# ScalarE's copies of a run's sums come three steps sooner in its order, in both scan layers

## The reference

```python
def step(hst, inp):                       # layer 1, 32 states; layer 3 has 64
    dt_t, B_t, C_t, x_t = inp
    dA = jnp.exp(dt_t[:, :, None] * A)
    hst = hst * dA + dt_t[:, :, None] * B_t[:, None, :] * x_t[:, :, None]
    y = jnp.einsum('bdn,bn->bd', hst, C_t)
    return (hst, y)
_, ys = jax.lax.scan(step, h0, seq)       # once forwards, once backwards in time
y = jnp.swapaxes(ys, 0, 1) + Dp * x
return y * _silu(z) @ out_proj_W          # then residual, layer norm, MLP
```

## Time and profile before

| | |
|---|---|
| median of 3 runs | 4702.95 us (4702.31 to 4705.61) |
| the profiled execution's own time | 4704.16 us |
| its span, first to last instruction | 4702.4 us |
| busy: PE, DVE, ACT, POOL | 4441.0, 4156.6, 4096.6, 3930.7 us |
| mean granted PE clock | 0.982 of full speed |
| scans on DVE (L1974) | 3072, 1.20 us each |
| products on POOL (L2341) | 768, 4.57 to 4.58 us each |

### The profile page before, as it was taken

How to read it: one execution, slowest core, us unless ns; L and a number is a source line. 1 busy time by engine, 2 the same in 40 slices (tenths; PEclk the granted TensorE clock), 3 DMA queues, 4 the chain that set the end, 5 groups by cost and what they waited for, 6 DMA issues and landing times.

```text
span 4702.4 us, 83409 instructions
## 1 busy us (share of the span) xinstructions
PE 4441.0 (94%) x32940; PEld 3730.5 (79%) x32940; DVE 4156.6 (88%) x4037; ACT 4096.6 (87%) x6807; POOL 3930.7 (84%) x1046
## 2 busy tenths in 40 slices
PE   8989899899899998999999999999999999999998
PEld 4458788778788884458888888888888888888887
DVE  6668999999899986759999999999998999999997
ACT  3459899899899974459999999999999999999996
POOL 4429899889889984539999998999998999989996
PEclk8999999999999999999999999999999999999999
DMA  3001111111111121011121211211211212111111
GB/s 125 1 15 51 50 47 51 46 46 51 46 46 50 51 68 39 1 39 54 57 75 54 77 50 52 78 57 54 79 55 46 80 59 76 54 50 65 56 59 41
DMA packets 90085, 252.74 MB, mean 54 GB/s; under 512 B 12240, under 2 KB 26448, under 8 KB 89696
## 3 DMA queue, kind: packets, MB, share of 16 engines
q1 hardware_dynamic: 89696, 247.40, 15.2%
HBM read 243.70 MB, written 3.67 MB: 53 GB/s over the span
## 4 chain that ended last, share of the span: by engine, by line
PE 47%; ACT 35%; DVE 8%; POOL 6%; issue 4%; DMA 0%; DVEq 0%; SPq 0%; POOLq 0%; ACTq 0%
PE psum L1015 12%; ACT weights_c L1528 9%; PE psum L748 9%; PE psum L1001 9%; ACT work L1528 7%; ACT work L1543 7%; PE psum L998 7%; ACT weights_c L1543 5%; PE psum L1115 5%; POOL work L2341 4%; DVE work L1974 3%; ACT L1316 2%; PE psum L1191 1%; DVE weights_c L1974 1%; ACT weights_c L1545 1%
## 5 line engine op out<-in xcount | busy, mean ns | idle before, releaser
L2341 POOL TENSOR_TENSOR work<-work,weights_a 128x2048 f32<-128x2048 f32 x512 | 2331.7, 4574 | 281.2 <-DVE work L1974 279.5
L1974 DVE TENSOR_TENSOR_SCAN work<-weights_c,psum 128x512 f32<-128x512 f32 x1366 | 1571.0, 1201 | 115.2 <-PE psum L1001 99.0
L1015 PE MATMUL psum<-ident,work 128*128 128x128 f32 x8192 | 1239.3, 275 | 12.9 <-ACT weights_a L1342 8.3
L2341 POOL TENSOR_TENSOR weights_c<-weights_c,weights_a 128x2048 f32<-128x2048 f32 x256 | 1168.3, 4580 | 73.9 <-DVE weights_c L1974 73.4
L1528 ACT ACTIVATE work<-work,decay 128x504 f32<-128x504 f32 x1366 | 965.5, 707 | 52.0 <-DVE work L1974 22.8
L1015 PEld LDWEIGHTS psum<-ident,work 128*128 128x128 f32 x8192 | 971.0, 143 | 14.8 <-ACT weights_a L1342 9.2
L1001 PE MATMUL psum<-ident,work 128*128 128x128 f32 x5464 | 937.8, 274 | 0.0
L1974 DVE TENSOR_TENSOR_SCAN work<-work,psum 128x512 f32<-128x512 f32 x682 | 789.8, 1200 | 40.9 <-PE psum L1001 28.1
L1974 DVE TENSOR_TENSOR_SCAN weights_c<-work,psum 128x512 f32<-128x512 f32 x684 | 792.0, 1200 | 37.7 <-PE psum L1001 36.9
L1001 PE MATMUL psum<-ident,weights_c 128*128 128x128 f32 x3752 | 696.9, 275 | 0.0
L1001 PEld LDWEIGHTS psum<-ident,work 128*128 128x128 f32 x5464 | 672.5, 143 | 0.0
(11 more groups left out here) (192 smaller groups left out, 6393.8 us busy)
## 6 DMA issues: line engine op xcount, KB each, us to landing
weights_a<-c_rows SPq DMA_DIRECT2D x384, 512.0 KB, 3.6
weights_c<-in_L_cond_fwd_in_w SPq DMA_DIRECT2D x8, 512.0 KB, 6.4
weights_c<-in_L_cond_fwd_xproj_w SPq DMA_DIRECT2D x4, 1024.0 KB, 7.3
weights_c<-in_L_cond_bwd_in_w SPq DMA_DIRECT2D x8, 512.0 KB, 5.8
weights_c<-in_L_cond_bwd_xproj_w SPq DMA_DIRECT2D x4, 1024.0 KB, 7.8
x_stream<-in_x_t SPq DMA_DIRECT2D x4, 512.0 KB, 8.6
weights_a<-in_L_cond_w SPq DMA_DIRECT2D x2, 1024.0 KB, 15.0
weights_a<-in_L_cond_W SPq DMA_DIRECT2D x2, 1024.0 KB, 8.0
```

The source lines that it names most:

```text
L1015: last = nc.tensor.matmul(PS[:, t, j * P:(j + 1) * P], buf["ring"][s % RING][:, j, t * P:(t + 1) * P], IDENT[:, :], start=begins, stop=((s ...
L1974: v.tensor_tensor_scan(buf["ring"][s % RING][:, j, along], buf["decay"][q % DECAYS][:, along], PS[:, 4 + q % LOOKAHEAD, along], 0.0, ALU.mult,
L2341: g.tensor_tensor(state, state, buf["c"][:, s // 2 % 2, s % 2, :].unsqueeze(1).broadcast_to([P, DC, T]), ALU.mult).then_inc(ss["prod_ready ...
```

## The change

One number: the step at which ACT's copies are due goes from 9 to 6. DVE's copies stay at 9, and so does PE's order.

```diff
                 def copy_sums(r, yt, done):
-                    yield 9
+                    yield 6
                     made("pe", f"dtx3@{r - 2}")
                     act.wait_ge(ss["sum_done"], r * pl.states)
                     for t in (0, 1):
```

## The result

The changed kernel takes 4692.69 us (median of 12 runs, 4692.13 to 4694.78) where the kernel before, on the same chip and beside it, took 4703.53 (12 runs, 4702.11 to 4709.89). The ratio is 0.9975, with a 95% interval of 0.9967 to 0.9984: 10.84 us, 0.23%. The forecast was 4691, in a range of 4686 to 4698.

The account below looks back on a forecast made before the run. PE's waits for ACT's copies at four layer 3 boundaries stall DVE, which sets the pace: 13.4 us back, less 1.4 for PE's clock, other places nothing, makes 12.0 off the median of 4702.95, near 4691 us; range 4686 to 4698.

Parts of the forecast that it names:

- The four places: Layer 3, runs 1, 2, 4 and 6, where PE waits for ACT's copies: 13.4 us back, 1.4 staying, 12.0 gained.
- The new waits of ACT: Before its moved copies ACT waits 1.8 us in three layer 1 runs, 2.9 in three of layer 3; costed at nothing.
- A fall at three of the four places: PE's clock falls after its remaining 1.84 us gap at three layer 3 boundaries, 0.45 us each, 1.4 us kept lost.
- The rule of the Trainium skill: Short idle gaps between bursts of matmuls keep PE's clock up; if it held, nothing would stay and the gain be 13.4.
- POOL: Rival: POOL, busy without a break through the boundary, sets the pace; gain some 2.5 us, 4700 us; 10%.
- The lead in the ring of states: Reason against POOL: four states and late adds let DVE run some microseconds ahead of it without waiting.
- PE does stay slow: Rival: the clock falls at scan 10 anyway, later stalls of 2.2 us stay in runs 2, 4, 6; 4696 us; 15%.
- ACT starving the scans: Rival: in layer 1 and layer 3's odd runs the new wait outlasts its cover; 15 us slower, 4718; 4%.
- The factor of 1: Whatever idle time DVE does not lose at a boundary is won whole by the next boundary, microsecond for microsecond.
- cover 1.5 us: Layer 1: the input of step 16 is complete at 1060.0, PE wants it at 1061.5, so ACT's new wait costs nothing.
- ACT makes the 1.8 us good: Layer 1: ACT later idles before decays that wait for a scan, and recovers its new 1.8 us wait there.

Follow-up runs that it names:

- the four places alone: The changed kernel with ACT's copies at step 6 only in runs 1, 2, 4 and 6 of layer 3, step 9 elsewhere: 4692.99 us, ratio 0.9975.
- run 4: No follow-up kernel: a stretch of one layer, from its scan 0 to the next run's; in layer 3, 333.78 us before, 331.53 changed.
- step 7: The changed kernel with ACT's copies due at step 7 instead of 6: 4692.82 us, ratio 0.9976 to the kernel before.
- run 2: No follow-up kernel: a stretch of one layer, scan 0 to next scan 0; layer 1 169.67 us before, 170.91 changed; layer 3 335.51 before, 333.05 changed.
- step 3: The changed kernel with ACT's copies due at step 3 instead of 6: 4713.03 us, ratio 1.0021 to the kernel before.
- step 5: The changed kernel with ACT's copies due at step 5 instead of 6: 4697.9 us, ratio 0.9987 to the kernel before.
- three copies on ACT: The changed kernel with ACT copying three of the four banks and DVE one: 4684.14 us, ratio 0.9957 to the kernel before.
- run 0: No follow-up kernel: a stretch of one layer, from its scan 0 to the next run's; in layer 3, 307.96 us before, 308.25 changed.

## Why the prediction was right

**Where the gain is.** The four places were named, and the kernel with those four alone has the whole gain. DVE's lost time there was put at 13.4 us with 1.4 staying, so 12.0; from scan 9 to scan 18 the four places give 11.85 (2.4, 3.4, 2.8 and 3.3). Where PE's clock did not fall there (runs 1, 2 and 6 as with the four places alone, run 4 as in the changed kernel), they give 13.7 against the 13.4 that were worked out.

**The new waits of ACT.** 1.8 and 2.9 us were worked out; 1.74, 1.86 and 1.86 were read in the three runs of layer 1, and 2.90 in layer 3, run 3, where DVE's own copies still wait 1.99 as in the earlier trace rows:

```profile
3047.50 1.08 ACT L1342 ACTIVATE weights_a<-psum 128x512 f32<-128x512 f32 x2 [2.90 <-PE psum L1015]
3047.51 1.29 DVE L1750 COPY weights_a<-psum 128x512 f32<-128x512 f32 x2 [1.99 <-PE psum L1015]
```

**PE's clock.** The windows over 6.5 us from scan 10 on, as in the earlier trace rows: the changed kernel in layer 1, runs 2 and 4, and layer 3, runs 2 and 4.

```profile
688.70:695.20 6.50, 5.22 (x31) 5.12 (x32) 6.50 (x7) 6.50 (x12) 6.50 (x3) 0.74 0.24 81
1054.40:1060.90 6.50, 5.22 (x31) 5.13 (x32) 6.38 (x7) 6.50 (x12) 6.50 (x3) 0.74 0.21 80
2713.80:2720.30 6.50, 5.21 (x32) 5.21 (x33) 6.40 (x7) 6.50 (x13) 6.50 (x3) 0.74 0.23 71
3367.80:3374.30 6.50, 5.19 (x43) 4.84 (x44) 6.50 (x7) 6.50 (x13) 6.50 (x3) 1.00 0.24 71
```

Each has the gap of 1.84 us. In three the mean granted clock is 0.74, partly at 1.2 GHz; in the fourth it is 1.00, 2.4 GHz throughout. A fall at three of the four places of layer 3 was forecast at 0.45 us each, and there it was at three (runs 1, 2 and 6), 0.6 us each against kernels that have none there (13.63 against 13.02, 12.82 against 12.20). That the number was three is luck. The prediction read a fall in two of three runs of layer 1 as a rate; with the four places alone, and with step 7, the same gaps brought one at one of the four places, and other orders have it at others. Layer 1, run 2 got a fall that it did not have before, which with 0.1 in run 4 is the 0.67 us that layer 1 lost and that the prediction had at zero. And the term was too small: by the end of the run a fall cost 1.5 and 1.4 us in runs 2 and 6 of layer 3 (run 1 shows no such cost).

The rule of the Trainium skill that was weighed there (page "TensorE: Matmul & The Clock Gate", section "Why this matters for your kernels") would have left no fall if a gap of this length counted as short; three windows in four speak against that. The prediction also counted the stall of run 2 before the change for the rule, but its two gaps, 1.84 and 1.94 us, are hardly longer than the 1.84 of layer 1. With gaps of at most 0.82 us, in the kernel whose DVE copies come a step later, the granted clock is 1.00 at all ten boundaries, which agrees with the rule.

**POOL.** The rows of POOL that answer to the earlier trace rows, layer 3, run 2:

```profile
2719.58 9.10 POOL L2341 TENSOR_TENSOR weights_c<-weights_c,weights_a 128x2048 f32<-128x2048 f32 x2
2728.64 9.09 POOL L2341 TENSOR_TENSOR work<-work,weights_a 128x2048 f32<-128x2048 f32 x2
```

Its 1.24 us of idle time are gone, so POOL is now busy throughout there, as that rival said. But DVE's gain was not taken back with it: run 2 is 2.46 us shorter, twice what POOL had idled, and kernels with one edit more are shorter again. The lead in the ring of states is what keeps POOL from setting the pace at this point; that is the prediction's reason, and only its outcome is shown.

**The other rivals.** PE does stay slow in part, but at 0.6 us a place and not at the 2.2 of that rival. ACT starving the scans is real at step 3, not at step 6.

**What was off.**

- *The factor of 1.* From DVE's copies to DVE's copies, run 2 to run 3 of layer 3, it is 3047.51 - 2712.62 = 334.89 us; 333.8 was forecast, from 337.34. The boundary of run 2 gave 3.43 and the run kept 2.46. Over layer 3, the sum of the lengths of runs 0 to 6 fell by 9.1 us against 11.85 at the boundaries: run 3 became 2.33 us longer, with 6.8 us at 1.2 GHz where before it had none. The other parts of the kernel gave 2.0 us net, among them 3.2 in layer 1, run 1, which is over before the first moved copy (10.2 us at 1.2 GHz instead of 17.1). So the 10.84 us are 11.85 from the mechanism and a remainder that happens to be small. The forecast's nearness to the total is partly luck; its nearness at the four places isn't.
- *The cover in layer 1.* The step "cover 1.5 us", at the input of step 16, was looked for at the wrong place. Between the copies and the Silu block ACT idled only 0.9 us in layer 1, run 2 before the change (0.15, 0.38 and 0.37, waits for scans). After it ACT does not idle there, so what is beyond those waits is carried to scan 32, whose decay had been ready 1.1 us before PE let the scan start. That is a cover of about 2 us, and two kernels bear it out: step 5 shows 2.95 - 0.7, about 2.3, and three copies on ACT show 1.74 + 0.49 of lateness less the 0.6 by which ACT came after PE, 1.7 us, with DVE 0.6 us ahead there because it makes one copy less. "ACT makes the 1.8 us good" was true by about half a microsecond. By the same argument step 5 would seem safe at the boundary, and there it was; further on it was not.
- *Step 5 isn't fully explained.* Against the changed kernel, its profile, which is of its slowest execution, has layer 1, run 1 at 188.4 and layer 3, run 0 at 309.6 where the changed kernel has 185.2 and 308.3. Neither run has a wait for ACT's copies. The first goes with 17.1 us at 1.2 GHz instead of 10.2; the second doesn't (6.8 and 6.7). What makes PE's clock fall in one execution or one kernel and not in another stays open, and no kernel here varied the clock alone.

## What to carry to other kernels

An instruction that another engine waits for should come up just as its own input is complete, no sooner: here one step late left half the wait, two steps of freedom (7 and 6) were equal, and three steps too early cost about twice what the move had gained. On an in-order engine with no idle time a new wait is carried past the place where it arises, so its cover has to be judged as far as the next long block on that engine, not only at the next few instructions. And once one engine's wait is gone, look at what the other one holds up at the same place: the copies on DVE, one step later, were worth as much again.

## What the runs showed of the hardware

PE's half speed costs through small things: four matmuls of an add take 1.06 to 1.12 us instead of 0.60 to 0.63, and while that lasts, scans wait 0.5 to 0.8 us each. A fall at a boundary cost 0.45 to 0.6 us by scan 18 and, but for layer 3, run 1, 1.1 to 1.5 us by the end of its run.

Whether a gap is followed by a fall can't be told from its length alone. In the eight profiles with PE's gap of 1.84 us as the only one at a boundary, the clock fell there at 18 of 39 places. In the five kernels with DVE's copies at step 10 or three copies on ACT, where no gap at a boundary is over 1.30 us, it fell at none of fifty. The two profiles of the changed kernel have their falls at the same boundaries, yet with the copies of other runs moved they come at others (layer 3, run 4 instead of runs 1, 2 and 6, with the four places alone). A run outside the move differs by up to 3.4 us from kernel to kernel (layer 1, run 1), and one kernel by up to 11.5 us between executions (step 5), the slower at a lower mean granted clock. So only the time at the place itself measures a small move.
